# Group norm behind the attention: statistics of 112 channels inside the attention's last five steps, of the last 16 channels from the block's tiles

## The reference

```python
scores = jnp.einsum('ncl,ncm->nlm', q, k) / jnp.sqrt(jnp.float32(c))
attn = jax.nn.softmax(scores, axis=-1)
right = jnp.einsum('nlm,ncm->nlc', attn, v)
out = xf.transpose(0, 2, 1) + right
return out.reshape(n, c, h, w)
...
m = jnp.mean(g, axis=(2, 3, 4), keepdims=True)
s = jnp.var(g, axis=(2, 3, 4), keepdims=True)
return ((g - m) / jnp.sqrt(s + eps)).reshape(v.shape)
```

## Time and profile before

| | |
|---|---|
| median of 3 runs | 4083.04 us (4076.82 to 4091.02) |
| the profiled execution | 4088.41 us, span of its instructions 4086.7 us |
| busy in the span: TensorE / VectorE | 84% / 79% |
| ScalarE / GpSimd | 48% / 55% |
| mean granted TensorE clock | 0.909 |

### The profile page before, as it was taken

How to read it: one execution, slowest core, us unless ns; L and a number is a source line. 1 busy time by engine, 2 the same in 40 slices (tenths; PEclk the granted TensorE clock), 3 DMA queues, 4 the chain that set the end, 5 groups by cost and what they waited for, 6 DMA issues and landing times. The chain is left out here.

```text
span 4086.7 us, 79072 instructions
## 1 busy us (share of the span) xinstructions
PE 3426.9 (84%) x28785; PEld 2168.6 (53%) x28785; DVE 3225.1 (79%) x6715; ACT 1954.3 (48%) x4385; POOL 2259.4 (55%) x2502
## 2 busy tenths in 40 slices
PE   4999968889999977979999976979999996883555
PEld 1666623447677742337767752335777762343444
DVE  5999867579999956659999957749999976755665
ACT  2444422346666632336666652345666653232333
POOL 3454550168878742038888835017887855006775
PEclk9999988989999988979999988989999998895556
DMA  1000002255555412055555521044555530127775
GB/s 50 9 12 12 27 16 51 66 154 149 154 154 148 125 37 50 1 170 153 151 150 152 150 61 43 8 129 142 156 152 146 155 95 18 44 63 209 220 218 175
DMA packets 219936, 426.59 MB, mean 104 GB/s; under 512 B 27825, under 2 KB 126540, under 8 KB 217512
## 3 DMA queue, kind: packets, MB, share of 16 engines
q0 software_dynamic: 92160, 302.06, 26.1%
q1 hardware_dynamic: 127346, 119.53, 10.2%
q10 hardware_dynamic: 54, 0.01, 0.0%
HBM read 340.77 MB, written 60.65 MB: 98 GB/s over the span
## 5 line engine op out<-in xcount | busy, mean ns | idle before, releaser
L1657 POOL TENSOR_TENSOR xl<-pt 128x192 bf16<-128x192 f32 (+1 forms) x1024 | 688.8, 674 | 425.0 <-PE bank L551 209.1
L878 ACT ACTIVATE pt<-bank 128x512 f32<-128x512 f32 x1024 | 608.8, 595 | 576.4 <-PE bank L520 344.9
L1646 POOL DMA_INDIRECT G<-patch_table,idx x576 | 593.9, 1031 | 162.8 <-issue 110.8
L551 PEld LDWEIGHTS bank<-vt,pt 128*128 128x128 bf16 x8192 | 550.0, 98 | 243.1 <-ACT pt L878 3.9
L1209 DVE TENSOR_REDUCE mxc<-bank 128x1 f32<-128x512 f32 x896 | 607.6, 679 | 37.4 <-PE bank L478 35.0
L551 PE MATMUL bank<-vt,pt 128*128 128x129 bf16 (+1 forms) x8192 | 634.3, 221 | 1.1 <-ACT osb L886 1.1
L1269 DVE TENSOR_TENSOR xl<-pt 128x320 bf16<-128x320 f32 (+1 forms) x1024 | 501.1, 490 | 72.3 <-PE bank L551 54.3
L551 PE MATMUL bank<-vt,xl 128*128 128x129 bf16 x4096 | 401.9, 221 | 12.7 <-DVE xl L1269 12.6
L1623 POOL TENSOR_TENSOR rs<-ve,mhalf 128x4 f32<-128x4 f32 x32 | 34.3, 1071 | 623.2 <-ACT ve L1005 623.2
L478 PE MATMUL bank<-reg,qh 128*128 128x512 bf16 x896 | 345.2, 386 | 12.0 <-DVE mxc L1209 8.5
L691 PE MATMUL bank<-reg,val 128*32 128x512 bf16 x3264 | 275.0, 399 | 65.4 <-DMA G<-xl 65.4
(11 more groups left out here) (248 smaller groups left out, 7020.2 us busy)
## 6 DMA issues: line engine op xcount, KB each, us to landing
patch_table<-valt SPq DMA_DIRECT2D x64, 512.0 KB, 7.0
G<-patch_table,idx POOLq DMA_INDIRECT x576
x_cur<-in_x SPq DMA_DIRECT2D x4, 2048.0 KB, 9.3
xl<-in_x SPq DMA_DIRECT2D x32, 256.0 KB
attn_out<-ob SPq DMA_DIRECT2D x32, 256.0 KB, 2.3
x_store<-x_cur SPq DMA_DIRECT2D x4, 2048.0 KB, 6.2
xr<-x_store SPq DMA_DIRECT2D x32, 256.0 KB
out<-fo SPq DMA_DIRECT2D x32, 256.0 KB
```

The source lines that it names most:

```text
L551: last = mm(O[t // 2][:, c0:c0 + width], image[:, at % ring, t * 128:(t + 1) * 128], vhl[:, values, st, 0:width], start=(st == 0 and part ...
L878: A(pt[:, at % PT_RING, :], ST[at % ST_RING] if n else ST_FIRST[at % 3], ACT.Exp, scale=SCALE).then_inc(s["exp_done"], 1)
L1646: g.indirect_dma_start(out=patches(j, k), out_offset=None, in_=table[:], in_offset=bass.IndirectOffsetOnAxis(ap=idx[:, j * K1 + k:j * K1 + ...
L1657: g.tensor_tensor(pl[:, at % PL_RING, 0:stop], pt[:, at % PT_RING, 0:stop], ph[:, at % PT_RING, 0:stop], ALU.subtract).then_inc(s["pl_p"], 1)
```

## The change

For the group norm behind the attention alone, the statistics are taken in two parts.

- Two memsets in step 249 clear a 128x128 tile (`by_group`, in the patch buffer `G`, whose slot is free by then) and four columns of `gst` for the last partitions.
- In steps 251 to 255 VectorE takes `bn_stats` of the first 112 channels (`FULL`), 2, 2, 2, 1 and 1 chunks a step, after it has waited for the first of the two loads. Their aggregate stands before the last `normalize`.
- The last 16 channels are not read from `x_cur` for this. The tile `ob` holds them as four pieces of 128 rows by 128 values; a piece is 4 channels, so one group. VectorE takes `bn_stats` of each piece along its rows and an aggregate of each (`tmv`: a mean and a variance for each row and piece).
- TensorE averages the row means of a piece over its 128 rows with `cavg` (all entries 1/128), for the deviations. For the groups' averages VectorE spreads the four columns over the last 16 columns of `by_group`, each four times, and TensorE adds a matmul that has `by_group` as its weights to the one with `gavg`, into the same accumulator.
- ScalarE waits for the second load before it writes `xn`; VectorE does not wait for it any more.

```diff
+STATS_AT = {-5: (0, 1), -4: (2, 3), -3: (4, 5), -2: (6,), -1: (7,)}
+        tst = sb("tst", [128, TB, 6])
+        tmv = sb("tmv", [128, TB, 2])
+        tdv = sb("tdv", [128, TB])
+        FULL = C - C // NCH
+        by_group = slots[:, 0, 0:128]
+        last_groups = by_group[:, FULL:C].rearrange("p (t r) -> p t r", r=GROUP)
...   TensorE
+            def group_norm_of_attention(gi):
+                pe.wait_ge(s["gn_stats"], gi + 1)
+                mm(O[0][:, 1:1 + TB], cavg[:], tmv[:, :, 0], start=True, stop=True)
+                mm(O[0][:, 0:1], gavg[:], gst[:, 0:1], start=True, stop=False)
+                mm(O[0][:, 0:1], by_group, cavg[:, 0:1], start=False, stop=True).then_inc(s["gn_grp"], 1)
+                pe.wait_ge(s["gn_dev"], gi + 1)
+                mm(O[1][:, 0:1], gavg[:], gst[:, 3:4], start=True, stop=False)
+                mm(O[1][:, 0:1], by_group, cavg[:, 0:1], start=False, stop=True).then_inc(s["gn_grp"], 1)
-                group_norm(4 * n + 1)
+                group_norm_of_attention(4 * n + 1)
...   ScalarE, behind the attention
+                act.wait_ge(s["r_in"], 32 * (n + 1))
                 group_norm(4 * n + 1)
...   VectorE, in the attention's loop over the steps
+                    if at == STEPS - 7:
+                        v.memset(by_group, 0.0)
+                        v.memset(gst[96:128, 0:4], 0.0)
+                    if at == STEPS - 5:
+                        dve.wait_ge(s["r_in"], 32 * n + 16)
+                    if at >= STEPS - 5:
+                        for c in STATS_AT[at - STEPS]:
+                            v.bn_stats(bst[0:FULL, c, :], x_cur[0:FULL, c * CH:(c + 1) * CH])
...   VectorE, behind the loop
+                dve.drain()
+                v.bn_aggr(gst[0:FULL, 0:2], bst[0:FULL].rearrange("p c s -> p (c s)"))
                 normalize(n, NCH - 1, 0)
                 normalize(n, NCH - 1, 1)
-                dve.wait_ge(s["r_in"], 32 * (n + 1))
-                for c in range(NCH):
-                    chunk_stats(c)
+                dve.drain()
+                for t in range(TB):
+                    v.bn_stats(tst[:, t, :], ob[:, t * 128:(t + 1) * 128])
+                dve.drain()
+                for t in range(TB):
+                    v.bn_aggr(tmv[:, t, :], tst[:, t, :])
+            def group_norm_of_attention(gi):
+                dve.drain()
+                v.tensor_copy(last_groups, per_group(tmv[:, :, 0]))
+                dve.drain()
+                dve.sem_inc(s["gn_stats"], 1)
+                dve.wait_ge(s["gn_grp"], 2 * gi + 1)
+                v.tensor_tensor(tdv[:], tmv[:, :, 0], O[0][:, 1:1 + TB], ALU.subtract)
+                v.tensor_tensor(gst[:, 2:3], gst[:, 0:1], O[0][:, 0:1], ALU.subtract)
+                v.tensor_copy(gst[:, 7:8], O[0][:, 0:1])
+                dve.drain()
+                v.tensor_tensor(tdv[:], tdv[:], tdv[:], ALU.mult)
+                v.scalar_tensor_tensor(gst[0:FULL, 3:4], gst[0:FULL, 2:3], gst[0:FULL, 2:3], gst[0:FULL, 1:2],
+                                       ALU.mult, ALU.add)
+                dve.drain()
+                v.tensor_tensor(tdv[:], tdv[:], tmv[:, :, 1], ALU.add)
+                dve.drain()
+                v.tensor_copy(last_groups, per_group(tdv[:]))
+                dve.drain()
+                dve.sem_inc(s["gn_dev"], 1)
+                dve.wait_ge(s["gn_grp"], 2 * gi + 2)
...   epsilon, power and bias as in group_norm
```

More of the change, by code:

```diff
@@ L1324, in attention, with per_group @@
                             dcn_finish((n - 1) * NCH + j // TB)
+                dve.drain()
+                v.bn_aggr(gst[0:FULL, 0:2], bst[0:FULL].rearrange("p c s -> p (c s)"))
                 normalize(n, NCH - 1, 0)
                 normalize(n, NCH - 1, 1)
-                dve.wait_ge(s["r_in"], 32 * (n + 1))
-                for c in range(NCH):
-                    chunk_stats(c)
+                dve.drain()
[4 more added lines that the diff above has]
+                    v.bn_aggr(tmv[:, t, :], tst[:, t, :])
+            def per_group(values):
+                return bass.AP(values.tensor, values.offset, [values.ap[0], values.ap[1], [0, GROUP]])
+            def group_norm_of_attention(gi):
[18 more added lines that the diff above has]
+                dve.wait_ge(s["gn_grp"], 2 * gi + 2)
+                v.tensor_scalar(gst[:, 4:5], O[1][:, 0:1], 1e-5, None, ALU.add).then_inc(s["gn_ve"], 1)
+                dve.wait_ge(s["gn_pow"], gi + 1)
+                v.tensor_scalar(gst[:, 6:7], gst[:, 7:8], gst[:, 5:6], -1.0, ALU.mult, ALU.mult)\
+                    .then_inc(s["gn_ready"], 1)
             def layer1(n):
```

## The result

| | before | after |
|---|---|---|
| median, runs | 4087.66 us, 5 (4076.82 to 4091.02) | 4055.73 us, 5 (4049.03 to 4064.12) |
| ratio after to before | | 0.9928 (0.9908 to 0.9948) |
| the profiled execution, its span | 4088.41, 4086.7 us | 4055.73, 4054.0 us |
| mean granted TensorE clock | 0.909 | 0.914 |

The changed kernel is 31.9 us faster by these medians; 25.5 were forecast. That the times agree so much better than the savings is chance: the median of the kernel before moved up by 4.6 us with its later runs.

What follows compares the result with a forecast made beforehand. A chain of waits between each sample's attention and layer 1 bounds the kernel; samples 1 to 3 save 6.6 us each, sample 0 5.7, together 25.5, giving 4057.5 us against the median 4083.04; range 4047 to 4071.

Steps and rivals of the forecast that it cites:

- Path two: VectorE, TensorE and GpSimd work from R, the start of the last normalize's reciprocal, to `xn`: ends at R+8.7, deciding.
- the four aggregates: On VectorE after the tile statistics, four aggregates of 6 values: 0.9 us, between 0.6 and 1.5.
- The four statistics: On VectorE after the last normalize, four statistics of 128 columns: 0.9 us, between 0.6 and 2.4.
- The first matmul group: TensorE's first answer in the group norm, three matmuls instead of one: 0.62 + 1.0 us.
- The added matmuls: Extra group-norm matmuls on TensorE: 0.5 us each, at most 0.62, at least nothing that shows.
- VectorE's part between the groups: VectorE's steps between the two matmul groups: 0.57 us before, 1.21 with four small instructions added.
- the DMA round trip decides: Rival: small instructions cost lower bounds, ScalarE waits for the reload until R+8.02; 28.3 us saved, 4055; chance 0.16.
- its variant without a shift of R: The round-trip rival with R, the last reciprocal's start, moved by nothing as well: 33 us saved, 4050.
- the case that I gave 0.67: The main forecast: path two decides at R+8.7, together 25.5 us saved, 4057.5 us.
- R moved: Statistics in the last five attention steps delay the last reciprocal: 1.0 us in samples 1 to 3, 2.3 in sample 0.
- the sum of full lengths on VectorE, 8.3: Samples 1 to 3, last five steps: `low_values`, `dcn_finish`, statistics, aggregate and gaps, ending at 1459.5 where R was 1458.52.
- The slower rival: Early load of 112 channels comes late, VectorE stalls in step 251: at 30 us flight 9.6 slower, 4093; chance 0.04.

Runs made afterwards that it cites:

- the short chain: Changed kernel with one round of matmuls for means and mean squares together, in place of means and then deviations; reload kept: 4059.35 us.
- the timed kernel of the spread statistics: Changed kernel with sample 0's eight statistics one in every second step, 239 to 253; timed in five rounds: 4051.69 us, ratio 0.991.

## Why the prediction was right, and where it was off

- **What bounds it.** Right: the stretch is a chain, and what left it came off the span one for one (31.4 by the stretches, 32.7 by the spans). The two halves run alone agree: with the reload alone off VectorE's side the chain is 13.2, with the 112 channels' statistics alone moved ahead it stays at 16.2, and with both it is 8.
- **Path two, 8.7.** The mechanism was right, the sum too large: 8.03, 7.73, 7.67 and 7.97 in samples 0 to 3. The term that was mis-sized in every sample is the four aggregates: 0.9 in the sum, 0.38 measured, below the 0.6 that I had called the lower end. I had multiplied one instruction's length, and instructions that do not wait for one another overlap. The four statistics, 0.9, came to 0.87. The first matmul group, from TensorE's start to VectorE, was put at 1.62: it took 1.47 in sample 3 and 0.86 in sample 1, at the two clock levels shown above. The added matmuls start 0.43 to 0.44 behind the one ahead in sample 3 and 0.23 to 0.24 in sample 1, where I had put 0.5. VectorE's part between the groups, put at 1.21, took 1.23 in sample 3 and 1.59 in sample 1, where 0.43 of idle time has no releaser in the trace; its cause is open.
- **VectorE: DVE Perf Modes**, as weighed in the prediction: in the Trainium skill's section on the trn2 errata the fixed latency is per instruction, and its form, which it gives for a `tensor_tensor` addition, makes an estimated 0.16 and 0.29 us of an aggregate and a 128-column statistic. The trace has 0.18 and 0.29 for the first of a row, 0.149 and 0.276 for the others. In a row they take less than four times that, 0.38 and 0.87, because each starts 0.08 before the end of the one ahead. So the form is right for one instruction and too dear for several in a row.
- **Which path decides.** Wrong by a hair: I named VectorE at R+8.7 with the reload 0.7 ahead of it. The reload ended last in three samples of four, by at most 0.28. Sample 0, where the drain plays no part, shows the tie best: 8.03 without the reload, 8.13 with the short chain, 6.91 with both. It hangs on small things: in the timed kernel of the spread statistics, whose samples 1 to 3 run the same code, VectorE ends last in sample 1, at 8.34. In the changed kernel the rival "the DMA round trip decides" had the better place, at 7.8 to 8.2, and the better sum too: 31.4 came, 28.3 was the rival's, 33 its variant without a shift of R, and 25.5 mine. It did not come by the rival's own condition, a path two of 6.6. So the case that I gave 0.67 named the wrong path in three samples, and the case that I gave 0.16 named the right one there.
- **R moved.** 1.0 was forecast in samples 1 to 3 and 0.10 came. The step that failed is the sum of full lengths on VectorE, 8.3: from the `low_values` at 1444.06, which is the one of 1451.21 in the earlier trace rows, to the reciprocal it came to 7.41. The statistics were priced right (4.88 for 4.85 in the sum). Four `low_values` took 1.58 from start to start and not 1.96, and the aggregate 0.29 and not 0.37, since an instruction that does not wait for the one ahead starts 0.08 before its end. `dcn_finish` took 0.59 from start to start, 0.67 to its end, where the earlier trace rows have 1.00; in that step GpSimd's `low_values` took the longer instead (two take 2.05 together). TensorE was not late at all: its last products start 24.01 us behind the load's issue, before and after. In sample 0 2.3 was forecast and 1.78 came, all of it through TensorE, whose two waits are 1.29 of it. Gaps of TensorE in the last five steps were a sign of being wrong in the prediction, and in sample 0 it was: the sum had VectorE come late by itself, and it is TensorE that ends late.
- **GpSimd beside the statistics.** No row shows harm. Of the pair at 1447.18 in the changed kernel the second `low_values`, by itself, lies wholly beside statistics and takes 0.51, no more than the shorter of the two lengths in the prediction:

```profile
1448.24 1.28 DVE L1338 BATCH_NORM_STATS2 bst<-x_cur 112x6 f32<-112x512 f32 x2
1448.73 0.51 POOL L1717 TENSOR_TENSOR xl<-pt 128x192 bf16<-128x192 f32 x1
```

  That agrees with the Trainium skill's SBUF — State Buffer, on who interferes with whom. The first of the pair takes 1.50; it lies beside `dcn_finish` and VectorE's own `low_values`, and both of these have two SBUF inputs, the case that this section of the Trainium skill names.
- **The slower rival** was mispriced. "Each us of lateness is a us of the span" does not hold for the first five: three tiles of low halves lie ahead of TensorE. Behind them it does hold (0.74 for 0.74). Its chance of 0.04 would have been lower with that seen.
- **Given back?** No: layer 1, from X to the next `xn`, takes 85.2, 85.5, 84.6 and 84.7 before and 85.1, 85.4, 85.1 and 84.9 after. That the rest of the span, 4021.2 and 4022.0, agrees within 1 us is partly chance: in the runs that keep GpSimd's drain it lies between 4015 and 4026.

The 31.9 against 25.5 is thus two terms: the chain (33.5 against the forecast's 7.6 x 3 + 8.0 = 30.8) and R (2.1 against 5.3). Both errors went the same way. That the time still came within 1.8 us of the forecast is luck with the median of the kernel before.

## What to carry to other kernels

Where a result must go through memory to change its layout, look whether its statistics can be had in the layout it has: they cost four statistics, four aggregates, five other small instructions and three small matmuls here, against 4.85 us behind a round trip of 6.6. A chain of waits often has several paths of nearly one length; before shortening one, take each away in turn, and then both, since the next wait (here a drain) shows only when both are gone. Removing a wait that was hidden is no gain in itself: what it waited for can come up later where nothing hides it.

## What the runs showed of the hardware

- A GpSimd drain behind the attention of samples 1 to 3 lasts 9.0 us (9.00, 8.98), and moves whole to the next drain if the first is left out. Before the change it was hidden: the power came after 17.28 us idle. In the changed kernel it comes after 9.05 in sample 1 and 9.00 in sample 2, where the drain already holds it: it starts 0.21 behind the end of VectorE's step, and 0.08 in the other samples. The reload hides that. That the gathers cause the drain's length is inferred from their absence in sample 0; no run here took them away.
- 256 KB from SBUF to SBUF in four transfers, each into four partitions, takes longer than a store to memory and a reload: the chain was 9.3 to 9.7 with it and 7.8 to 8.2 without. Store and reload in two halves are slower as well, 8.4 to 9.25, in the one kernel that has them.
- `bn_stats` of 512 columns takes the same on 32, 112 and 128 partitions (4.86, 4.84, 4.85 for eight).
- In these rows a VectorE instruction that waits for nothing starts 0.08 us before the end of the one ahead, whatever its length: statistics of 512 columns are 0.68 long and start 0.60 apart, those of 128 columns 0.276 and 0.193, aggregates of 6 values 0.149 and 0.066.
